# GNN stack on one core: the next layer's virtual-node row begun between the matmuls of this layer, and layer-norm variances taken tile by tile

## The reference

```python
h = genconv(h0 + vn, gcn_W[0], gcn_b[0])
for l in range(1, 7):
    h2 = relu(ln(h, norm_g[l-1], norm_b[l-1]))
    vn_tmp = sum_over_nodes(h2) + vn
    vn_hid = relu(ln(vn_tmp @ vn_W1[l-1] + vn_b1[l-1], vn_g[l-1], vn_beta[l-1]))
    vn = vn_hid @ vn_W2[l-1] + vn_b2[l-1]
    h2 = h2 + vn
    h = genconv(h2, gcn_W[l], gcn_b[l]) + h
h = ln(h, norm_g[6], norm_b[6])

def genconv(h, W, b):
    msg = relu(h[src]) + 1e-7
    ex = exp(msg - segment_max(msg)[dst])
    agg = segment_sum(msg * ex) / segment_sum(ex)
    return (h + agg) @ W + b
```

## Time and profile before

| | us |
|---|---|
| median of three executions | 936.58 |
| lowest and highest | 935.05, 938.19 |
| the profiled execution | 937.22 |
| its span, first to last instruction | 935.4 |
| TensorE busy, weight loads busy | 776.1, 494.1 |
| VectorE busy | 617.5 |
| ScalarE, GpSimd busy | 225.9, 144.8 |

### The profile page before, as it was taken

The page is one execution under the profiler, slowest core; times in us unless marked ns, Lnnn a source line. Parts: engine busy times, 40 slices in busy tenths (PEclk is TensorE's granted clock), DMA queues, the critical chain, the costliest instruction groups (busy, mean ns, idle before and its releaser), DMA issues.

```text
span 935.4 us, 10162 instructions
## 1 busy us (share of the span) xinstructions
PE 776.1 (83%) x2750; PEld 494.1 (53%) x2750; DVE 617.5 (66%) x1576; ACT 225.9 (24%) x449; POOL 144.8 (15%) x153
## 2 busy tenths in 40 slices
PE   6587797887775999999999987146978988979998
PEld 2345365455354756657567552135466475665663
DVE  8765675676675533533643533199999999998980
ACT  6522111112111222221232211400601503406300
POOL 6000000000001000000000000730181081340000
PEclk9789989999997999999999989579998999999999
DMA  6712214124221323333232100750351243130000
GB/s 209 268 57 90 99 47 146 61 85 146 86 87 48 131 78 121 132 107 107 101 113 95 57 1 23 218 209 1 157 145 59 117 141 147 34 102 1 0 1 22
DMA packets 35905, 89.97 MB, mean 96 GB/s; under 512 B 3570, under 2 KB 3967, under 8 KB 35231
## 3 DMA queue, kind: packets, MB, share of 16 engines
q1 hardware_dynamic: 30752, 72.81, 21.8%
q0 software_dynamic: 5120, 16.78, 6.0%
HBM read 88.53 MB, written 1.05 MB: 96 GB/s over the span
## 4 chain that ended last, share of the span: by engine, by line
PE 34%; issue 30%; DVE 21%; DVEq 9%; POOL 2%; ACT 2%; DMA 1%; POOLq 0%; ACTq 0%; SPq 0%
PE PS L741 23%; DVE big L1356 7%; DVEq L1350 6%; PE PS L968 4%; DVE tail L1366 4%; PE PS L982 3%; PE PS L750 2%; POOL rstd L532 1%; DVE tail L1375 1%; DVE prods L1375 1%; ACT big L622 1%; POOL big L552 1%; DVEq L1356 1%; DVEq L1351 1%; PE PS L829 1%
## 5 line engine op out<-in xcount | busy, mean ns | idle before, releaser
L741 PE MATMUL PS<-big 128*128 128x512 f32 (+1 forms) x368 | 136.2, 523 | 8.1 <-DVE big L1186 5.6
L1366 DVE SCALAR_TENSOR_TENSOR tail<-big,coef 128x448 f32 (+2 forms) x220 | 139.3, 635 | 0.0
L1356 DVE TENSOR_TENSOR big<-big,tail 128x448 f32 (+2 forms) x220 | 127.3, 579 | 7.1 <-DVE tail L1366 4.5
L741 PEld LDWEIGHTS PS<-big 128*128 128x128 f32 x368 | 67.9, 190 | 71.2 <-issue 67.4
L552 POOL DMA_INDIRECT big<-h_rows,src_i x64 | 87.0, 1359 | 83.5 <-PE PS L968 60.6
L532 POOL TENSOR_TENSOR rstd<-var,minus_half 128x1 f32<-128x1 f32 x38 | 28.7, 765 | 457.1 <-DVE var L1024 457.1
L741 PE MATMUL PS<-hT,big 128*128 128x256 f32 x384 | 84.9, 381 | 4.2 <-ACT hT L653 4.2
L741 PEld LDWEIGHTS PS<-hT,big 128*128 128x128 f32 x384 | 72.3, 190 | 15.5 <-issue 3.9
L968 PE MATMUL PS<-big,hotd_more 128*128 128x512 f32 x176 | 76.3, 592 | 0.0
L1042 DVE TENSOR_TENSOR h<-PS,h 128x512 f32<-128x512 f32 x26 | 17.9, 690 | 79.7 <-PE PS L741 79.7
L982 PE MATMUL PS<-xn,tail 128*128 128x256 f32 x104 | 29.8, 436 | 40.0 <-DVE tail L1375 40.0
(11 more groups left out here) (190 smaller groups left out, 1062.9 us busy)
## 6 DMA issues: line engine op xcount, KB each, us to landing
big<-in_L_gnn_vn_W_dram SPq DMA_DIRECT2D x12, 1024.0 KB, 5.2
big<-in_edge_attr_dram SPq DMA_DIRECT2D x3, 3584.0 KB, 10.6
big<-in_L_gnn_m_w_dram SPq DMA_DIRECT2D x8, 1024.0 KB, 5.3
big<-in_L_gnn_gcn_W_dram SPq DMA_DIRECT2D x7, 1024.0 KB, 5.2
big<-in_L_gnn_wv_dram SPq DMA_DIRECT2D x4, 1024.0 KB, 5.3
big<-in_L_gnn_wq_dram SPq DMA_DIRECT2D x4, 1024.0 KB, 5.2
big<-in_L_gnn_wk_dram SPq DMA_DIRECT2D x4, 1024.0 KB, 5.4
big<-in_L_gnn_wo_dram SPq DMA_DIRECT2D x4, 1024.0 KB, 5.3
```

The costliest lines, as they stand in the source:

```text
L741: return pe.matmul(o, lhsT, rhs, start=start, stop=stop)
L1356: dve.tensor_tensor(o, o, prod[:, row % RING, 0:n, :], ALU.add)._wait_ge(path_step, g * STEPS + 2 * row + 1).then_inc(path_step, 1)
L1366: dve.scalar_tensor_tensor(out=prod[:, row % RING, 0:n, :], in0=xs[:, :, bass.ds(i1, EXT)], scalar=coef[:, row:row + 1], in1=xe[:, :, bass ...
```

## The change

The row's bank becomes bank 7, and both halves of the turned `md` go to bank 6 (`MD`). TensorE's program of a layer changes in these places, for every layer that has one behind it (0 to 5): the bias product of the *next* layer stands behind the products with `vhid`, and the first of the four products of the new `vn` with the next `W1` stands behind the transposes of `md` half 0. Three of those products are left at the top of the layer. The transposes of `md` half 1 also wait until VectorE has read half 0 (`mex_ready`), since both use bank 6. The last layer is written out behind the loop, without the parts for a next layer. On VectorE each tile's mean and variance are taken directly behind its statistics, in the layer before, instead of both at the start of the layer.

```diff
--- before.py
+++ after.py
@@ -85,7 +85,7 @@
 OUT_L2, OUT_L3 = LN_L1_IN + 1, LN_L1_IN + 2
 
 TR_L2 = LAYERS
-VN_HIDDEN, VN_OUT = 6, 2
+VN_HIDDEN, VN_OUT, MD = 7, 2, 6
 
 
 class Steps:
@@ -619,7 +619,7 @@
                                            accum_out=hsum[:, c:c + 1]).then_inc(hT_ready, 1)
                 for b in range(2):
                     act.wait_ge(mdT_done, l * 2 + (b + 1))
-                    act.activation(ex[:, :, b * N:(b + 1) * N], halves(6 + b), ACT.Exp, bias=zero).then_inc(ex_ready, 1)
+                    act.activation(ex[:, :, b * N:(b + 1) * N], halves(MD), ACT.Exp, bias=zero).then_inc(ex_ready, 1)
                 for b in range(2):
 
                     act.wait_ge(den_done, l * 2 + (b + 1))
@@ -632,7 +632,7 @@
             layer0(0, True)
             act.wait_ge(cond_b, 1)
             for g in range(4):
-                act.activation(condT[32 * g:32 * g + NC, :], PS[0:NC, 7, 0:N], ACT.Identity, bias=fb[:, 1:2]).then_inc(cond_set, 1)
+                act.activation(condT[32 * g:32 * g + NC, :], PS[0:NC, MD, 0:N], ACT.Identity, bias=fb[:, 1:2]).then_inc(cond_set, 1)
             with act.Fori(1, LAYERS) as l:
                 steps.enter(l - 1, 2)
                 layer0(l, False)
@@ -794,20 +794,23 @@
                     if o % 2:
                         ins.then_inc(done, 1)
 
-            def layer0(l, first):
-                def column(col, c):
-
-                    return col[:, c:c + 1].to_broadcast([P, P])
-
+            def column(col, c):
+
+                return col[:, c:c + 1].to_broadcast([P, P])
+
+            def vn_hidden_bias(l):
+                pe.wait_ge(b1_in, 16)
+                mm(PS[:, VN_HIDDEN, :], ones[0:1, :], b1_rows[:, bass.ds(l * D - D, D)], True, False)
+
+            def vn_hidden_part(l, lo, hi):
+                pe.wait_ge(w_in[1], l * 16)
+                pe.wait_ge(vn_set, l * 2 - 1 if hi <= 2 else l * 2)
+                for c in range(lo, hi):
+                    mm(PS[:, VN_HIDDEN, :], column(vn, c), wbuf[1][:, c, :], False, False)
+
+            def layer0(l, first, last):
                 if not first:
-
-                    pe.wait_ge(b1_in, 16)
-                    mm(PS[:, VN_HIDDEN, :], ones[0:1, :], b1_rows[:, bass.ds(l * D - D, D)], True, False)
-                    pe.wait_ge(w_in[1], l * 16)
-                    if True:
-                        pe.wait_ge(vn_set, l * 2)
-                    for c in range(CT):
-                        mm(PS[:, VN_HIDDEN, :], column(vn, c), wbuf[1][:, c, :], False, False)
+                    vn_hidden_part(l, 1, CT)
                 turn(l, ln_out, l * 2)
                 if not first:
                     for c in range(CT):
@@ -821,12 +824,16 @@
                             ins = mm(PS[:, VN_OUT + b, 0:N], column(vhid, c), wbuf[2][:, c, b * N:(b + 1) * N],
                                      c == 0, c == CT - 1)
                         ins.then_inc(vn_half, 1)
+                if not last:
+                    vn_hidden_bias(l + 1)
 
                 def turn_md(b):
                     pe.wait_ge(md_ready, l * 2 + (b + 1))
+                    if b:
+                        pe.wait_ge(mex_ready, l * 2 + 1)
                     for c in range(2):
                         for t in range(NT):
-                            ins = pe.transpose(halves(6 + b)[:, t, c * P:(c + 1) * P],
+                            ins = pe.transpose(halves(MD)[:, t, c * P:(c + 1) * P],
                                                md[:, 2 * b + c, t * P:(t + 1) * P], ident[:])
                     ins.then_inc(mdT_done, 1)
 
@@ -838,6 +845,8 @@
                     ins.then_inc(done, 1)
 
                 turn_md(0)
+                if not last:
+                    vn_hidden_part(l + 1, 0, 1)
                 gather(0, ex, ex_ready, den_done, 0)
                 turn_md(1)
                 gather(2, mex, mex_ready, num_done, 0)
@@ -854,13 +863,14 @@
                             ins.then_inc(conv_done, 1)
 
             pe.wait_ge(cols_set, 2)
-            layer0(0, True)
+            layer0(0, True, False)
 
             pe.wait_ge(cond_s, 1)
-            mm(PS[0:NC, 7, 0:N], fw2[:], cz, True, True).then_inc(cond_b, 1)
+            mm(PS[0:NC, MD, 0:N], fw2[:], cz, True, True).then_inc(cond_b, 1)
             pe.wait_ge(cond_set, 4)
-            with pe.Fori(1, LAYERS) as l:
-                layer0(l, False)
+            with pe.Fori(1, LAYERS - 1) as l:
+                layer0(l, False, False)
+            layer0(LAYERS - 1, False, True)
 
             def table(i, b, t):
                 pe.wait_ge(tabw_in[i], b * 128 + 128)
@@ -1031,6 +1041,10 @@
 
                 for t in range(NT):
                     aggregate(n, t)
+                normalise_tiles(n, inp)
+
+            def normalise_tiles(n, inp):
+
                 for t in range(NT):
                     dve.wait_ge(ln_est, n * 2 + (t + 1))
                     dve.tensor_scalar(xn[:, t, :], inp[:, t, :], mv[:, t, 0:1], rstd[:, t:t + 1],
@@ -1113,7 +1127,7 @@
             dve.tensor_scalar(cz, PS[0:NC, 6, 0:N], fb[:, 0:1], None, ALU.add).then_inc(cond_z, 1)
 
             def layer0(l, first):
-                layer_norm(l, x if first else h)
+                normalise_tiles(l, x if first else h)
                 dve.wait_ge(hT_ready, l * CT + CT)
                 def par(name, at=0, n=CT):
                     return cols[:, bass.ds(l * CT + (COL[name] - CT + at), n)]
@@ -1159,7 +1173,7 @@
                     half = slice(b * N, (b + 1) * N)
                     dve.wait_ge(mdT_done, l * 2 + (b + 1))
                     dve.wait_ge(ex_ready, l * 2 + (b + 1))
-                    dve.tensor_tensor(mex[:, :, half], halves(6 + b), ex[:, :, half], ALU.mult).then_inc(mex_ready, 1)
+                    dve.tensor_tensor(mex[:, :, half], halves(MD), ex[:, :, half], ALU.mult).then_inc(mex_ready, 1)
 
                 def shifted(b):
                     for c in (2 * b, 2 * b + 1):
@@ -1201,6 +1215,8 @@
                     ins.then_inc(bias_added, 1)
                     dve.wait_ge(bias_added, 1)
                     take_stats(h)
+                    for t in range(NT):
+                        aggregate(1, t)
                 else:
                     dve.wait_ge(w_in[0], l * 32 + 32)
                     carry()
@@ -1208,9 +1224,12 @@
                     dve.wait_ge(bias_added, l + 1)
                     for t in range(NT):
                         residual(t, 4, conv_done, l * 2, h)
+                        aggregate(l + 1, t)
 
             dve.wait_ge(x_in, 16)
             take_stats(x)
+            for t in range(NT):
+                aggregate(0, t)
             layer0(0, True)
             with dve.Fori(1, LAYERS) as l:
                 steps.enter(l - 1, 30)
@@ -1218,7 +1237,7 @@
             steps.leave(LAYERS - 1)
 
 
-            layer_norm(LN_L0_LAST, h)
+            normalise_tiles(LN_L0_LAST, h)
             dve.wait_ge(ln_out, LN_L0_LAST * 2 + 2)
             dve.wait_ge(gb_in, 32)
             for k, op in ((0, ALU.mult), (1, ALU.add)):
```

## The result

The changed kernel takes 930.30 us in the median of five executions (925.47 to 932.62), against 936.58 before: a ratio of 0.9934, 95% interval 0.9914 to 0.9953. It is faster by 0.66%, 6.3 us. The record holds five executions of the kernel before, not three, with the same median. The profiled execution took 932.62 us, the slowest of the five; its span is 930.8 us.

What follows compares the result with a forecast made beforehand. No engine alone was the bound: TensorE and VectorE hand work to each other. Gains of 8.25, 1.9 and 0.35 less costs of 3.7, 1.0, 0.4 and 3.6 gave -1.8 us: 934.8 us from the 936.58 median, range 930.5 to 938.5.

Steps and rivals of the forecast that it cites:

- The top of a layer: Fewer products ahead of the top transposes: 1.65 us gained in each of layers 2 to 6, 8.25 us in all.
- The shared bank: Second transposes of `md` waiting for `mex` half 0 in the shared bank: no cost, margin over 1 us.
- the weights: The next `W1` lands at 224.6, TensorE needs it at about 227.6: no cost.
- The norm behind layer 6: No TensorE work stands ahead of this norm, so earlier variances gain 0.35 us.
- A layer at full clock: Sign to check: a layer with the clock up should take 33.2 us instead of 34.17.
- The bias behind `vhid`: Delays the transposes of `md`: 0.5 us at full clock, 0.8 where it fell, 3.7 us cost in all.
- The clock fell in five layers of six: Clock low behind `vhid` in five of six layers instead of three; two more falls cost 3.6 us.
- layer 0, its transposes to its last product: Added product at half clock ahead of layer 0's first gather: cost 0.4 us, between 0.95 cost and 0.6 gain.
- top of layer 1, first record to the transposes: Two products fewer with the clock low there: 1.9 us gained, 3.4 if the clock doesn't fall.
- product behind the transposes of `md`: One product in the 0.78 us gap takes 0.2 us too much: 1.0 us cost in five layers.
- The rival in which the clock falls no oftener: No more clock falls than now, so the 3.6 us cost goes away: 931.2 us, chance 0.25.
- its second figure (929.7): No more clock falls than now, and the clock also up at the top of layer 1: 929.7 us.

Runs made afterwards that it cites:

- e1: The kernel before with seven idle products behind the products with `hsum` in layers 1 to 6: 934.53 us, ratio 0.9971.
- e3: The kernel before with only the mean and variance taken tile by tile at the layer's end: 937.31 us, ratio 0.9989.
- e2: The changed kernel with seven idle products behind the products with `hsum` in layers 1 to 6: 926.39 us, ratio 0.9882.
- e4: The changed kernel with the variances taken at the start of the layer again, so only the products' placement changes: 940.20 us, ratio 1.0026.
- e7: The changed kernel with variances back at the layer's start, plus seven idle products behind the products with `hsum`: 925.80 us, ratio 0.9903.
- e9: The changed kernel, unaltered, measured once more on another chip: 936.51 us, ratio 0.9966 to the kernel before.
- e10: Repeat of the changed kernel with variances back at the layer's start, nothing filled: 943.06 us, ratio 1.0033.
- e8: The changed kernel, bias behind the last gather, idle products behind `hsum`, in layer 0 and behind layer 6: 918.37 us, ratio 0.9819.
- e5: The changed kernel with the bias product moved from behind `vhid` to behind the last gather, nothing filled: 928.80 us, ratio 0.9935.
- e6: The changed kernel with the bias behind the last gather and seven idle products behind the products with `hsum`: 923.83 us, ratio 0.9874.

## Why the prediction was wrong

**What held.** The top of a layer: 1.65 us forecast for layers 2 to 6, 1.3 to 1.45 measured, plus 0.1 for the hand-over from the layer before. The transposes came to wait for VectorE. The shared bank and the weights cost nothing: in layer 5 the second transposes start 1.83 us after the first gather in both kernels (225.73 - 223.90, and 229.81 - 227.98 before), and the product with `vn`, which takes the next `W1`, starts at 222.96 with no idle time before it. The norm behind layer 6 gave its 0.35 us. A layer at full clock took 33.29 us, 33.2 forecast. The bias behind `vhid` is not in a gap: 0.66 us at full clock where I had 0.5. The clock fell in five layers of six.

**The step that failed: the low clock of layer 0 and of the top of layer 1 was taken from the trace before as given.** In the profiled execution the first network became 4.5 us shorter where the sum said 1.8. The terms of the sum, beside what the two traces show:

| us | forecast | measured |
|---|---|---|
| start of layer 0 | not in the sum | -0.7 |
| layer 0, its transposes to its last product | +0.4 | -1.1 |
| top of layer 1, first record to the transposes | -1.9 | -3.6 |
| tops of layers 2 to 6 | -8.25 | -7.2 |
| `vhid` to `md`: bias and falls of the clock | +3.7 + 3.6 | +8.5 |
| product behind the transposes of `md` | +1.0 | 0.0 |
| behind the last product of layer 6 | -0.35 | -0.4 |
| sum | -1.8 | -4.5 |

Layer 0: I took a cost of 0.4, the ends being -0.6 and 0.95. The product did delay the gather, by 0.7 us, but with it the clock was up at 46 us instead of 50.3. Top of layer 1: I took the clock as low, and named 3.4 us for the case that it isn't; it was up, and the transposes started 2.67 us after the first record instead of 6.27. Together these two terms were to give 1.5 us and gave 4.7. The other traces bear this out. From the transposes of layer 0 to those of layer 1, the three kernels with nothing added to layer 0 (before, e1, e3) take 34.9, 35.8 and 36.2 us. The six with the bias and the product in layer 0 (the change, e2, e4, e7, e9, e10) take 30.0 to 30.2 us four times and 33.0 and 31.9 twice; in these two the clock was low at the top of layer 1 again. That the added products are what brings the clock up sooner fits this, and in e8, with idle products in layer 0 as well, the clock was up all through it and the same stretch takes 28.3 us; but no run added them to layer 0 alone, so this cause is argued and not shown.

The product behind `md` was mis-sized too, by 1.0 us. Against these, two terms were too good: the tops by 1.05 us, and `vhid` to `md` by 1.2 (38.0 - 29.5 = 8.5, forecast 7.3). How these 8.5 us divide is not settled by the pair of traces. With 0.66 us for each of five biases, 5.2 are left for two more falls; but e5 against layer 5 of the change shows 1.1 us for a bias where the clock fell, where I had 0.8, and with 0.66 + 4 x 1.1 (an estimate from these two) 3.4 are left, close to my 3.6. The 0.8 took TensorE as never idle ahead of those transposes where the clock fell; in layer 3 of the kernel before it was idle there for 0.28 us. The 0.7 us at the start of layer 0 are chance: over all kernels its transposes start between 36.1 and 37.0 us, in the two traces of the changed kernel at 36.19 and 36.88.

**What failed, in the median.** Of the 4.5 us by which the forecast missed, 2.8 lie in the profiled execution (935.4 forecast, 932.6 measured); the other 1.7 are no term of the sum. I set the offset of the profiled execution to the median (0.64 us) as if it were the kernel's own. The profiled execution of the changed kernel is 2.3 us *above* its median. The executions of the change scatter over 7 us, and the mean granted clock on record for each goes with it: 0.933 in the slowest (932.62), 0.939 in the fastest (925.47), with the others in order between. In e9 it is 0.925 in the slowest of twelve (940.73) and 0.938 in the fastest (931.12). Which stretches were low in the executions without a trace isn't known. That scatter was missing from the range: I built it from cases of the clock, but centred it on one execution, and it began at 930.5 though one of its own cases stood at 929.7.

The rival in which the clock falls no oftener (931.2) gives a time nearer to the result, but not its reason: behind `vhid` it fell oftener. The clock up at the top of layer 1, which its second figure (929.7) adds, did come. There is chance in the miss as well: the repeat (e9, ratio 0.9966) would be 933.4 us on a kernel before of 936.58, inside the range. So the size of this gain is itself known to some 3 us only.

## What to carry to other kernels

Look for TensorE's idle time ahead of a hand-over and ask what clock follows it. Here the same kernel, with idle products in that time, gained 0.3% (e1), and 0.5% on top of the change (e2), about what the change of the order gave by itself (0.34 to 0.66%). Compare two orders with the clock held up; without that, 0.16 us in a layer went with 0.7% in the time. And when a change adds work to a stretch in which the clock is low, don't take the low clock as given: here that was the largest error of the forecast. Measure a gap against the work that is to go into it: behind `vhid`, 0.31 us of idle time couldn't hide a bias product, while ahead of the layer's product 0.86 us hid all but 0.1 of it.

## What was not expected

The fourth network, the same in all kernels, took from 349.8 to 356.6 us (table), more than most of the differences under study; the second and third, from the end of the first to the start of the fourth, took 299.7 to 302.1 us in all. The traces give a lead. Summed over windows of 0.25 us, the granted clock was low for 67 to 68 us of the fourth network in the five kernels before, the change, e2, e6 and e8, which took 350.0 to 350.4 us there. In the other eight it was low for 72 to 82 us, and seven of them took 351.8 to 356.6 (e7 is the exception, 74 us low and 349.8). What makes the clock differ there was not followed up. Where a change touches one stage only, the end of that stage in the trace leaves the other stages out: e3's first network ends 2.5 us sooner than before, e3's fourth takes 6.6 us longer, and its time says "same". But the end of the stage holds the clock too: e3's `vhid` to `md` is 2.6 us shorter because the clock fell in two layers instead of three, and only 0.35 us were expected of the edit. The length of one layer at full clock is the measure that the clock leaves alone.

An idle product is not harmless by itself: fourteen records take 3.19 us at full clock, and records of that size take nearly twice as long at the low clock, 3.78 us for eight against 1.99. In e8 they came while the clock was up; what they do where it is low already was not tried.
